# Row operations moved between VectorE, GpSimd and PSUM in a fused attention and expert kernel

## What is computed

```python
mod = (_silu(c) @ wmod).reshape(32, 6, 1, -1)
sa, ca, ga, sb, cb, gb = (mod[:, j] for j in range(6))
ga = (2 * (ga >= 0) - 1) * jnp.maximum(jnp.abs(ga), 0.25)   # gb alike
h = _layernorm(x) * (1 + ca) + sa
x = x + ga * attention(h, rot_w, scale, bias)
h = _layernorm(x) * (1 + cb) + sb
x = x + gb * experts(h, gate_w, Wg, Wu, Wd, Ws_g, Ws_u, Ws_d)
# attention: q, k, v = rotations of h; attn = softmax((2 + 2 q.k) / scale + bias)
#   ave = attn @ v; out = ave / sqrt(max(|sum(ave * ave)|, 1e-8))
# experts: scores = softmax(h @ gate_w.T); topk_w, topk_idx = top_k(scores.T, 64)
#   routed: (gelu(x_tok @ Wg.T) * (x_tok @ Wu.T)) @ Wd.T * topk_w, added to the rows topk_idx
#   shared: (gelu(h @ Ws_g.T) * (h @ Ws_u.T)) @ Ws_d.T
```

## Time and profile before

| | us |
|---|---|
| median of the runs (lowest to highest of 3) | 2468.98 (2467.78 to 2469.15) |
| profiled execution | 2462.94 |
| its span, from the first instruction to the last | 2460.9 |
| attention phase, set-up included, to the first gathered rows of step 3 | 0 to 1350.64 |
| rest of the expert phase | 1350.64 to 2460.9 |

### The profile page before, as it was taken

The page is one execution under the profiler, slowest core; times in us unless marked ns, Lnnn a source line. Parts: engine busy times, 40 slices in busy tenths (PEclk is TensorE's granted clock), DMA queues, the critical chain, the costliest instruction groups (busy, mean ns, idle before and its releaser), DMA issues.

```text
span 2460.9 us, 40295 instructions
## 1 busy us (share of the span) xinstructions
PE 2298.0 (93%) x13548; PEld 1985.4 (81%) x13548; DVE 1639.7 (67%) x2972; ACT 1189.8 (48%) x2298; POOL 1385.4 (56%) x1157
## 2 busy tenths in 40 slices
PE   5899999899998999989888999999999999999997
PEld 3788888778786877878777888888888888888886
DVE  5678878788887888888857555555555555554553
ACT  3666666566565666656553333333333333333332
POOL 2465565555645455554544666666666666565664
PEclk9999999999999999999999999999999999999999
DMA  2111211122121111212124444444344444344433
GB/s 90 60 64 64 75 64 66 58 72 72 58 65 59 64 68 62 73 58 65 50 80 106 88 84 85 86 86 86 59 87 84 87 84 89 82 61 86 84 63 43
DMA packets 82967, 179.38 MB, mean 73 GB/s; under 512 B 12240, under 2 KB 47216, under 8 KB 82832
## 3 DMA queue, kind: packets, MB, share of 16 engines
q0 software_dynamic: 49152, 67.14, 16.8%
q1 hardware_dynamic: 33680, 110.27, 13.1%
HBM read 110.03 MB, written 67.34 MB: 72 GB/s over the span
## 4 chain that ended last, share of the span: by engine, by line
PE 46%; DVE 5%; issue 2%; POOL 2%; ACT 1%; DMA 1%; SPq 0%; DVEq 0%; ACTq 0%; POOLq 0%
PE ps L365 15%; PE ps L366 14%; PE ps L367 14%; PE ps L517 2%; DMA stage<-in_wd 1%; DVE neg_mean_rstd L974 0%; DVE hidden_f L936 0%; ACT pairs L667 0%; POOL hidden L1229 0%; POOL x_rows L1270 0%; PE ps L432 0%; DVE best_positions L1046 0%; DVE score_rows L1047 0%; DVE pairs L979 0%; DVE stage L984 0%
## 5 line engine op out<-in xcount | busy, mean ns | idle before, releaser
L365 PE MATMUL ps<-x_t,weights 128*128 128x512 f32 x1536 | 616.2, 401 | 16.0 <-issue 11.2
L1325 POOL DMA_INDIRECT out<-x_rows,step_token x256 | 418.4, 1634 | 327.7 <-DVE x_rows L1171 268.9
L366 PE MATMUL ps<-x_t,weights 128*128 128x512 f32 x1536 | 602.2, 392 | 0.0
L367 PE MATMUL ps<-x_t,weights 128*128 128x512 f32 x1536 | 601.4, 392 | 0.0
L365 PE MATMUL ps<-weights,hidden 128*128 128x256 f32 x2048 | 584.1, 285 | 9.9 <-POOL hidden L1229 6.4
L366 PE MATMUL ps<-weights,hidden 128*128 128x256 f32 x2048 | 580.8, 284 | 0.0
L367 PE MATMUL ps<-weights,hidden 128*128 128x256 f32 x2048 | 580.5, 283 | 0.0
L1192 DVE TENSOR_TENSOR hidden_f<-gelu,ps 128x512 f32<-128x512 f32 x256 | 175.5, 686 | 385.3 <-ACT gelu L787 385.2
L787 ACT ACTIVATE gelu<-ps 128x512 f32<-128x512 f32 x256 | 152.5, 596 | 544.1 <-PE ps L367 544.1
L365 PEld LDWEIGHTS ps<-weights,hidden 128*128 128x128 f32 x2048 | 392.9, 192 | 20.1 <-issue 8.1
L366 PEld LDWEIGHTS ps<-weights,hidden 128*128 128x128 f32 x2048 | 393.1, 192 | 7.4
(11 more groups left out here) (176 smaller groups left out, 3725.2 us busy)
## 6 DMA issues: line engine op xcount, KB each, us to landing
mod_b<-mod_rows SPq DMA_DIRECT2D x32, 640.0 KB, 5.8
x_rows<-in_x SPq DMA_DIRECT2D x32, 512.0 KB, 3.5
h_rows<-stage SPq DMA_DIRECT2D x32, 512.0 KB, 2.9
out<-y_rows SPq DMA_DIRECT2D x32, 512.0 KB, 2.6
stage<-in_wg SPq DMA_DIRECT2D x16, 512.0 KB, 3.8
stage<-in_wd SPq DMA_DIRECT2D x16, 512.0 KB, 6.8
stage<-in_wu SPq DMA_DIRECT2D x16, 512.0 KB, 5.3
sa_ca_b<-mod_rows SPq DMA_DIRECT2D x31, 256.0 KB, 4.9
```

The source lines that it names most:

```text
L365: pe.matmul(o, lhs(HI), rhs(HI), start=start, stop=False)
L366: pe.matmul(o, lhs(HI), rhs(LO), start=False, stop=False)
L367: return pe.matmul(o, lhs(LO), rhs(HI), start=False, stop=stop)
L1325: pool.indirect_dma_start(out=out_rows, out_offset=bass.IndirectOffsetOnAxis(ap=ICUR[g][:, t:t + 1], axis=0), in_=X1[:, g % 2, t * D:(t + ...
```

## The change

It does the following.

- *Norms.* L916 and L974 go from DVE to GpSimd: `rstd` makes minus mean first, then the power, then the product. The floor of `out_norm` (L940) goes to GpSimd as two rows (`floor_squares`); the maximum stays on DVE, behind the second half of the attention output instead of ahead of the subtraction that releases the keys (`h1_low`).
- *Gate.* The transposes of the gate's logits become products with a folding matrix, which adds the two halves; `gate_max` reads PSUM, and one row of DVE goes.
- *Top-k.* A round writes its values and positions in place; the copy and the index row of each round become one copy and one index row a group (`top_tokens`).
- *K.* Copy, subtraction and semaphores go by halves of 512 columns.
- *Loops.* The outer loop over two groups is written out on PE and DVE; on DVE the inner one too.
- *Set-up.* The rows of sequence 0 are standardised ahead of the copies of the first modulations and multiplied on DVE; the gate modulations are made in two halves in iteration -1, the statistics of sequence 1 move ahead of the softmax subtractions, the subtractions of the shared weights go to GpSimd, and in iteration 1 the softmax transposes go ahead of the second norm's.
- *GpSimd's order.* One of the two hidden subtractions that stood between residual and `rstd` goes ahead of the residual.

```diff
-            with e.Fori(0, 2) as g:
-                with e.Fori(0, GROUP // 2 - 1) as q:
+            for g in range(2):
+                if unrolled:
+                    for r in range(6):
+                        i = g * 8 + r + 11
+                        iteration(i, i % 2, i // 2, ((g, r, g * 8 + r),))
+                else:
+                    with e.Fori(0, GROUP // 2 - 1) as q:
...
                 for k in range(KD):
-                    mm = mm3(PC[:, (KD + k) * S:(KD + k + 1) * S], lambda a: ROTK[:, a, k, :],
-                             lambda a: H1_T[:, a, k, :], True, True)
-                mm.then_inc(k_done, 1)
+                    mm3(PC[:, (KD + k) * S:(KD + k + 1) * S], lambda a: ROTK[:, a, k, :],
+                        lambda a: H1_T[:, a, k, :], True, True).then_inc(k_done, 1)
...
-                    mm = pe.transpose(PD[:, 512 + t * 2 * E:512 + (t + 1) * 2 * E], GLT[:, t * P:(t + 1) * P],
-                                      IDENT[0:2 * E, 0:2 * E])
+                    mm = pe.matmul(PD[:, 512 + t * E:512 + (t + 1) * E], GLT[:, t * P:(t + 1) * P], FOLD[:, :],
+                                   start=True, stop=True)
...
+            def keys_hi(n):
+                for k in range(KD):
+                    act.wait_ge(k_done, n * KD + k + 1)
+                    act.copy(K_T[:, HI, k, :], PC[:, (KD + k) * S:(KD + k + 1) * S]).then_inc(k_hi, 1)
...
-                dve.scalar_tensor_tensor(ZZ[:, :], Z[:, :], 1e-8, Z[:, :], ALU.mult, ALU.mult).then_inc(zz_ready, 1)
                 dve.wait_ge(zz_ready, n + 1)
                 dve.wait_ge(ssq_done, (n + 1) * T)
                 dve.tensor_tensor(NSQ[:, :], ZZ[:, :], SSQ[:, :], ALU.max).then_inc(norm_sq, 1)
...
-                dve.tensor_reduce(GL[:, :, :], PD[:, 512:512 + T * 2 * E].rearrange("p (t a e) -> p t e a", t=T, a=2),
-                                  AX.X, ALU.add).then_inc(gate_sum, 1)
-                wait_apart(dve, gate_sum, n + 1)
-                dve.tensor_reduce(GMX[:, :], GL[:, :, :], AX.X, ALU.max).then_inc(gmax_ready, 1)
+                lg = PD[:, 512:512 + T * E].rearrange("p (t e) -> p t e", t=T)
+                dve.tensor_reduce(GMX[:, :], lg, AX.X, ALU.max).then_inc(gmax_ready, 1)
...
-                dve.tensor_copy(TOPV[:, :, bass.ds(r * 8, 8)], BESTV[:, :].unsqueeze(1).to_broadcast((P, 2, 8)))
-                wait_apart(dve, top_step, before * 3 + 3)
-
-                dve.tensor_scalar(TOPI[:, :, bass.ds(r * 8, 8)], BESTU[:, :].unsqueeze(1).to_broadcast((P, 2, 8)),
-                                  CONST[:, bass.ds(g + C_BASE, 1)], None, ALU.add).then_inc(top_kept, 1)
+                wait_apart(dve, top_step, before + 1)
+                best = TOPV[:, 0, r * 8:(r + 1) * 8]
+                dve.max_index(TOPU[:, r * 8:(r + 1) * 8], best, src[:, :])
+                dve.match_replace(dst[:, :], best, src[:, :], -1.0).then_inc(top_kept, 1)
+
+            def top_tokens(g):
+
+                dve.wait_ge(top_kept, (g + 1) * (CAP // 8))
+                dve.tensor_copy(TOPV[:, 1, :], TOPV[:, 0, :])
+                dve.tensor_scalar(TOPI[:, :, :], TOPU[:, :].unsqueeze(1).to_broadcast((P, 2, CAP)),
+                                  const(g + C_BASE), None, ALU.add).then_inc(top_index, 1)
...
                 wait_apart(pool, mv, n + 1)
+                pool.tensor_scalar(NMR[j][:, :], MV[j][:, :, 0], -1.0, None, ALU.mult)
                 pool.tensor_scalar(RS[j][:, :], MV[j][:, :, 1], EPS, None, ALU.add).then_inc(ve, 1)
                 pool.wait_ge(ve, n + 1)
                 pool.tensor_tensor(RS[j][:, :], RS[j][:, :], const(C_HALF, T), ALU.pow).then_inc(rs, 1)
+                pool.wait_ge(rs, n + 1)
+                pool.tensor_tensor(NMR[j][:, :], NMR[j][:, :], RS[j][:, :], ALU.mult).then_inc(nm, 1)
+
+            def shared_weights_lo(m):
+                pool.wait_ge(w_hi, m + 1)
+                cols = slice(m * WCOLS, (m + 1) * WCOLS)
+                pool.tensor_tensor(W[0][:, LO, cols], W_RAW[m], W[0][:, HI, cols].bitcast(F32),
+                                   ALU.subtract).then_inc(w_lo, 1)
+
+            def floor_squares(n):
+
+                wait_apart(pool, exp_done, (n + 1) * T)
+                pool.tensor_scalar(ZZ[:, :], Z[:, :], 1e-8, None, ALU.mult).then_inc(z_small, 1)
+                pool.wait_ge(z_small, n + 1)
+                pool.tensor_tensor(ZZ[:, :], ZZ[:, :], Z[:, :], ALU.mult).then_inc(zz_ready, 1)
```

More of the change, by code:

```diff
@@ L386, in _, with modulations, rotation_rows @@
                       start=True, stop=True).then_inc(row0_ps, 1)
-            def modulations():
+            def modulations(n):
                 pe.wait_ge(wmod2_in, 16)
[L391 to L394, removed]
+                for k in range(KD):
+                    mm = pe.matmul(PG[0:B, n * 512:(n + 1) * 512], CACT_T[:, k, :],
+                                   WMOD[:, k, 2 * D + n * 512:2 * D + (n + 1) * 512], start=k == 0, stop=k == KD - 1)
                 mm.then_inc(mods_ps, 1)
+            def rotation_rows():
                 pe.wait_ge(diag_ready, 1)
@@ L446, in a_times_v @@
                     if t == 2:
-                        wait(pe, gate_sum, n)
+                        wait(pe, gl_ready, n)
                     for q in range(T):
@@ L544, in iteration @@
                     down(i - 2)
+                if at(i, 1):
+                    a_transposes(1)
                 if valid(i - 1):
                     h2_transposes(i - 1)
-                if valid(i):
+                if valid(i) and not at(i, 1):
                     a_transposes(i)
@@ L741, in iteration @@
                                        accum_out=Z[:, t:t + 1]).then_inc(exp_done, 1)
-                if valid(i - 1):
-                    for k in range(KD):
-                        act.wait_ge(h2t_done, (i - 1) * KD + k + 1)
-                        act.copy(H2_T[:, HI, k, :], PG[:, k * S:(k + 1) * S]).then_inc(h2t_hi, 1)
+                if valid(i - 1) and not at(i, 1):
+                    h2_high(i - 1)
                 if valid(i):
@@ L1136, in iteration @@
                     attention_out(i, 0, p, half + 1)
-                if valid(i + 1) and not at(i, -1):
+                if valid(i + 1):
                     ln1_apply(i + 1, 1 - p)
@@ L1289, in iteration @@
                     v_low(i)
+                if at(i, 0):
+                    for m in range(3):
+                        shared_weights_lo(m)
                 if valid(i + 1):
-                    rstd(0, mv1, ve1, rs1, i + 1)
+                    rstd(0, mv1, ve1, rs1, nm1, i + 1)
+                if valid(i):
+                    floor_squares(i)
                 if at(i, B):
```

243 lines of the change are left out of this document (132 added, 111 removed).

## The result

The changed kernel takes 2361.14 us (median of 4 runs, 2360.59 to 2363.87), the kernel before 2469.07 beside it; the ratio is 0.9572, 95% interval 0.9558 to 0.9586. The forecast was 2365 (range 2346 to 2394). The profiled execution took 2360.59 us, its span 2358.7, 102.2 less than before.

A forecast was written before the change was run, and what follows sets the result against it. TensorE, busy 93% of the span, was taken as the bound, so only its idle time could be won; the stretches' gains summed to 104.3, and 2468.98 - 104.3 = 2365 us, range for 8 in 10 2346 to 2394.

The forecast's parts named there:

- The lock, and the second norm: GpSimd's lock on the shared port holds DVE's 2.35 us product; moving it brings rows net 1.75 earlier, no wait left.
- The first rival: Norm maximum still held on DVE, or a new wait at the second norm: 2385 to 2430 us, chance 18%.
- Gate from PSUM: Folding in PE's transposes of the same count drops one DVE row; hides nothing mid-stream, frees a row held 4.17 at i=32.
- What PE's work alone takes: An iteration without the four PE waits takes between 34.84 and 35.48 us; 35.2 taken.
- Norm maximum and top-k round: 3.3 to 4.6 us leave DVE ahead of the keys; waits of 1.09 and 0.41 vanish, two rounds should also fit.
- K by halves: Halving the keys' copy and subtraction takes over 1.1 us off the path, against the 0.69 wait before the scores.
- Hand-overs: At i=10, 18, 26, the 4.48 "issue" wait goes with the written-out loop; 3.2 kept at 18 and 26, 2.0 at 10.
- the clock: Allowance for TensorE's lower clock after a hand-over wait: 1.6 us at 18 and 19.
- Set-up: Up to the first gate product: 16.5 us gained, bounds 12 and 21; first scores near 27.8 instead of 33.80.
- End of the attention phase: 1220.49 to 1350.64: 4.5 us gained, between 0 and 7, from the held row, residual order, second norm and shorter rounds.
- The experts: Expert phase after 1350.64, touched by the change in its first three steps alone: no gain counted.

The follow-up runs named there:

- run 2: Changed kernel with the second norm's shift product back on VectorE, between the two pairs of score maxima; 2393.33 us, ratio 0.9695.
- run 3: As run 2, and GpSimd's subtraction of the values waits until the shift product is made; 2359.64 us, ratio 0.9558.
- run 10: Changed kernel with GpSimd's two hidden subtractions both between residual and power again; 2368.13 us, ratio 0.9598.
- run 1: Changed kernel with plain transposes for the gate, the halves added by a VectorE row; 2354.15 us, ratio 0.9544.
- run 4: Changed kernel with the attention norm's floor back on VectorE and, with the maximum, ahead of the subtraction that releases the keys; 2371.61 us, ratio 0.9611.
- run 7: Changed kernel with the copy and the index row of each top-k round back; 2377.93 us, ratio 0.9635.
- run 5: Changed kernel with the keys copied and subtracted whole again, ScalarE's copy still ahead of its scaling rows; 2365.32 us, ratio 0.9589.
- run 6: Changed kernel, keys by halves, but ScalarE scales the attention output's first half ahead of the keys' copies; 2379.18 us, ratio 0.9649.
- run 11: Changed kernel with TensorE's outer loop over two top-k groups back, VectorE's written out; 2367.96 us, ratio 0.9599.
- run 12: Run 8 plus score rows and slots ahead of the keys' subtraction, a delayed GpSimd weight subtraction, and iteration 1's second norm ahead of the later softmax half; 2322.69 us.
- run 8: Run 1 with TensorE's loop over the experts written out; 2336.10 us, ratio 0.9471.

## Why the prediction was right, and where it was so by luck

By the spans the change won 102.2 us against a sum of 104.3. That the time none the less came out 3.9 below the forecast has to do with the executions that were profiled: the one before was 6.1 under its median, a difference that the prediction left on both sides, and the one after only 0.6.

*The lock, and the second norm.* Right, and shown by runs 2 and 3. The rows came 0.65 ahead of PE (between 0.2 short and 1.1 to spare was said). Undone, the shift costs 1.24 an iteration (run 2), GpSimd's order 0.38 (run 10). The Trainium skill (SBUF — State Buffer, section "SBUF: two separate sides") says that whoever starts first keeps the shared port pair for the whole instruction; 2.36 against 0.16 agrees. The first rival (maximum still held) did not occur: 0.16. But the holding has moved rather than gone: GpSimd's subtraction of the values (522.89 to 525.30) now holds the second row of the softmax's biases, 1.6 us where the first row takes 0.29, in nearly every iteration. That costs PE nothing: no wait follows.

```profile
523.72 1.60 DVE L1017 TENSOR_SCALAR exp_bias<-neg_max,scale_bias 128x2 f32<-128x2 f32 x1
```

*Gate from PSUM.* This step failed. "PE's transposes of the same count" was costed at nothing; the four products with the folding matrix became eight rows, 0.99 from their start to the next row, where the transposes of the kernel before took 0.36, from 574.09 to 574.45:

```profile
574.09 0.43 PE L475 MATMUL ps<-consts,gate_logits_t 32*128 32x32 f32 x4
```

That is 0.63 us an iteration, 20 us in 32, and run 1 shows it. The Trainium skill has the rule that I should have weighed (Perfetto Trace Analysis, section "Transposes"): a transpose should be done as one, and not as a matmul. The trace agrees.

*What PE's work alone takes.* 35.2 was taken as 34.84 and some wait left; measured are 35.25, and no wait is left. The number was right by luck. The floor with plain transposes is 34.63 (run 1), 0.2 lower than 34.84: beside its tail of 0.16 each wait also lengthens the row behind it (0.47 against 0.39 before keys and scores, 1.09 and 1.06 against 1.03 and 1.04 at the transposes, 0.24 together). 34.63 + 0.63 = 35.26. So two errors, a floor too high and a cost left out, met in the right number. Without the fold, 35.2 would have been 0.6 too high.

*Norm maximum and top-k round.* Both waits went, as forecast, but the 3.3 to 4.6 us were more than was needed. With one round an iteration the floor alone can come back for nothing and the copies for 0.25 (runs 4 and 7); only with two rounds do they count (7.1 and 11.4 us in 26 to 30). So in 12 to 25 either of the two moves is nearly enough; both back together wasn't run.

*K by halves.* The wait went, but this step failed too: it gave the wrong reason. Halving is worth 0.15 an iteration (run 5). The move of ScalarE's scaling behind the copies, which neither the list of the change nor the prediction has, is worth 0.58 (run 6).

*Hand-overs.* 36.4 us in the three stretches against 34.9 forecast. The "issue" wait went with TensorE's loop (run 11); what is left, 2.9, fell to 0.24 when the copy stood ahead of DVE's attention rows and of the keys' subtraction (run 12). At 18 and 19 there was luck: 1.6 was counted for the clock, which then stayed at 1.00. In run 3, with the same hand-over and a wait of 2.88, it fell, and the stretch took 2.8 us more:

```profile
656.93:733.79 76.86, 73.92 (x444) 64.68 (x443) 57.65 (x122) 48.87 (x103) 43.46 (x41) 0.96 0.20 66
```

*Set-up.* 13.6 within bounds of 12 to 21. The queue of weight subtractions held one row, not the fold but the bias (2.39). First scores came at 25.07, sooner than 27.8, but such a lead is mostly waited away: in run 8, whose set-up differs by the gate alone, they came at 27.57 and the keys of i=2 at 90.14. Here 2.45 were lost again before the gate, where the second norm's rows now stand behind the softmax's. Run 12, with both edits at once, won 3.95 back.

*End of the attention phase* 2.8 against 4.5, in its bounds; which of its four terms fell short was not worked out. *The experts*, put at nothing, gave 2.1: the returns of the loop cost 9.0 instead of 13.0, and step 3 loses part of that again (19.27 instead of 17.66).

## What to carry to other kernels

Price what an edit adds to the engine that bounds, row by row, even where an instruction only changes its kind: here that was the dearest term left out, and undoing it and the loop's return (25 us, run 8) brought more than the waits that were left (13 us, run 12). A row that is long for its size may be held by another engine; to free it pays only where its engine does not idle soon behind it, so read the wait of the next rows first, and look for the row that will be held in its place. A total that fits does not show that its terms do: undo them one at a time, and compare the stretch, not the sum.

## What was not expected of the hardware

- The return of a loop cost TensorE 0.8 to 5.0 us where the body is eight expert steps, nothing visible where it is two attention iterations (35.25 and 35.26 an iteration, without waits), 4.0 to 4.5 where it is a whole group (6.94 less the 2.90 of the hand-over in run 11; 4.48 in the earlier trace rows). The expert loop's own code was the same each time; its six returns cost 7.2 to 9.2 us in all the runs with the fold, 12.4 and 13.0 in the two with the program before, 19.7 with plain transposes in the changed program. So it goes with the program ahead of the loop, most likely with TensorE's; by what, its length or its place, is open. Written out, it is zero (run 8). The Trainium skill (Runtime: NRT & Kernel Launch, section "Instruction fetch mechanics") says that a taken branch to a target outside the fetched window has to fetch first; the runs agree, and give the price. The queue that loads instructions (q8) shows the fetch: around the return at 1683.39 in run 1 it brings three loads within 11 us (1679 to 1690), at the same step of run 8 one in 19 us (1671 to 1690), and between 200 and 340 in the changed kernel, in the loop of two iterations, none. First run 1, then run 8 (loads, MB, share):

```profile
q8 instruction: 3, 0.05, 2.5%
```

```profile
q8 instruction: 1, 0.02, 0.4%
```

- TensorE's clock fell from 2.4 to 1.2 GHz after some waits and not after others as long: a granted clock of 1.00 behind the 2.90 at 692.87, 0.50 behind the 2.79 at 978.26. What decides is open. Stretches with length, PE's busy time and rows, clock, DMA share, GB/s:

```profile
692.87:694.00 1.13, 1.13 (x5) 1.00 0.00 0
...
978.20:980.00 1.80, 1.74 (x4) 0.50 0.00 0
```

- VectorE rows of 32x16 and 128x2 elements were held 2.34 and 2.39 us: here the length of a held row was set by the GpSimd row, whatever its own size.
